# A graph network kernel: the stages between and behind the edge passes cut into chunks of four blocks

## The reference

```
h    = x @ node_fc_W + b ;  gate = sigmoid(x @ gate_W + gate_b)
# layer 0, per edge: attention over h[src] . h[dst], three relation weights from edge features,
# softmax by destination, segment sums, then a product with folded weights:
h_red = relu(concat([h_att, h_rel]) @ out_fc_W + out_fc_b)
h_out = where(deg > 0, h_red, h)
x1    = layernorm(x + gate * h_out + (1 - gate) * x)
# layer 1, per edge: e = tanh(x1[src] @ Wq + x1[dst] @ Wk), score = e @ Wphi,
# alpha = exp(score - max) / (sum over src + 1e-9)
out   = layernorm(x1 + segment_sum(alpha * (x1[dst] @ Wy_w + Wy_b + e @ We), src))
```

## Time and profile before

| | us |
|---|---|
| median of 3 runs | 2567.0 (2566.91 to 2568.18) |
| the profiled execution, its own time | 2568.5 |
| its span in the profile | 2566.9 |
| busy: PE / DVE / ACT / POOL | 2112.0 / 1811.4 / 1533.1 / 1658.5 |

### The profile page before, as it was taken

How to read it: one execution, slowest core, us unless ns; L and a number is a source line. 1 busy time by engine, 2 the same in 40 slices (tenths; PEclk the granted TensorE clock), 3 DMA queues, 4 the chain that set the end, 5 groups by cost and what they waited for, 6 DMA issues and landing times. The chain is left out here.

```text
span 2566.9 us, 63030 instructions
## 1 busy us (share of the span) xinstructions
PE 2112.0 (82%) x16604; PEld 1421.1 (55%) x16604; DVE 1811.4 (71%) x6215; ACT 1533.1 (60%) x4445; POOL 1658.5 (65%) x1800
## 2 busy tenths in 40 slices
PE   5799999997999999999995757777777777777773
PEld 4333333332677777777775446556555555555551
DVE  7984556110788888888876548787888887878764
ACT  2466777776666777667762136666666666666641
POOL 1277777776777777777720057777777777777740
PEclk9999999999899999999997558898989888989885
DMA  9244444553777777777731022222222222222220
GB/s 94 60 142 131 132 132 133 150 141 96 213 202 197 202 203 201 201 201 202 200 102 35 28 62 80 79 78 79 79 79 79 79 78 79 79 78 78 79 50 25
DMA packets 213904, 297.98 MB, mean 116 GB/s; under 512 B 87552, under 2 KB 136597, under 8 KB 213808
## 3 DMA queue, kind: packets, MB, share of 16 engines
q0 software_dynamic: 78400, 180.35, 25.9%
q1 hardware_dynamic: 135408, 116.54, 17.9%
HBM read 238.46 MB, written 58.28 MB: 116 GB/s over the span
## 5 line engine op out<-in xcount | busy, mean ns | idle before, releaser
L1569 POOL DMA_INDIRECT sum_acc<-kv_table,rec_all x784 | 741.4, 946 | 239.1 <-issue 236.6
L1068 POOL DMA_INDIRECT area_b<-h_table,src_g x448 | 459.1, 1025 | 144.0 <-issue 126.6
L512 POOL DMA_INDIRECT early<-h_table,src_g x336 | 331.3, 986 | 222.2 <-ACT sum_acc L727 141.8
L727 ACT ACTIVATE sum_acc<-twin,bias 128x1024 f32<-128x1024 f32 x294 | 318.1, 1118 | 154.9 <-PE twin L597 151.1
L1655 ACT COPY sum_acc<-sum_acc 128x768 f32 x220 | 183.4, 833 | 307.6 <-POOLq L1575 189.5
L597 PE MATMUL twin<-area_b,wc 64*128 64x512 f32 x1176 | 313.6, 634 | 11.0 <-ACT sum_acc L727 11.0
L1141 PE MATMUL bank<-hs,y_sb 128*128 128x129 f32 x2344 | 311.2, 275 | 0.6 <-ACT y_sb L1164 0.6
L1141 PEld LDWEIGHTS bank<-hs,y_sb 128*128 128x128 f32 x2344 | 285.7, 192 | 1.3 <-ACT y_sb L1164 1.1
L1168 ACT COPY y_sb<-bank 128x512 f32<-128x512 f32 x293 | 171.8, 586 | 190.6 <-PE bank L1132 190.6
L1627 PE MATMUL twin<-sum_acc,probT 128*128 128x193 f32 x880 | 206.9, 387 | 27.5 <-DVE probT L1765 27.0
L1627 PE MATMUL bank<-sum_acc,probT 128*128 128x193 f32 x880 | 206.0, 385 | 25.0 <-DVE probT L1765 23.4
(11 more groups left out here) (311 smaller groups left out, 4685.5 us busy)
## 6 DMA issues: line engine op xcount, KB each, us to landing
hs<-rows_table SPq DMA_DIRECT2D x293, 258.0 KB
rows_table<-area_b POOLq DMA_DIRECT2D x112, 258.0 KB
area_b<-in_edge_attr SPq DMA_DIRECT2D x97, 256.0 KB, 2.9
rows_table<-early POOLq DMA_DIRECT2D x84, 258.0 KB
sum_acc<-kv_table,rec_all POOLq DMA_INDIRECT x784
...
```

The costliest lines, as they stand in the source:

```text
L512: pool.indirect_dma_start(out=early[:, g % RINGE, j, 0:D], out_offset=None, in_=h_table, in_offset=bass.IndirectOffsetOnAxis(ap=src_g[:, g ...
L727: act.activation(hid_words[:, first:first + 2 * GE], twin[p % 2][:, :], ACT.Relu, bias=bias1[:, m:m + 1]).then_inc(hid_sb, 1)
L1068: pool.indirect_dma_start(out=landed_rows[:, g % RINGE * GT + j, 0:D], out_offset=None, in_=h_table, in_offset=bass.IndirectOffsetOnAxis(a ...
L1569: pool.indirect_dma_start(out=landed_rows[:, g % RING1 * GT + j, :], out_offset=None, in_=kv_table, in_offset=bass.IndirectOffsetOnAxis(ap ...
```

## The change

The middle and the last stage are written as loops over seven chunks: six of four blocks and one of a single block. Work with a factor or an offset per lane (h by `held`, relu by `taken`, x1 = y by rstd plus shift, the accumulator by den) becomes ACTIVATEs on ScalarE, one for each block with the factor as a pointer operand (128x1). gate is now computed in the first stage with a Tanh instead of the Sigmoid, and x_sb is multiplied there by 2 - gate. The value's bias moves out of the middle stage: it is row 65 of the weights w_e1 of the last stage, whose input is the 65 columns from D on of acc_st (the last is the sum of the weights), so the products with one row of ones are gone. rescale works on 8 windows instead of 20. kv_table is written by pairs of blocks from four buffers. The clears of acc_st and top_st stand on GpSimd in the middle stage. The last stage takes its maximum from the running maximum of the last step instead of searching for it, and writes the output chunk by chunk.

```diff
-w_e1 = sb("w_e1", [AD, D])
+w_e1 = sb("w_e1", [AD + 1, D])
...
-        (w_kvq[:, KV:], i["L1_gnn_Wq"]), (b_kvq[:, AD:KV], row(i["L1_gnn_Wy_b"])),
-        (w_e1[:, :], i["L1_gnn_We"]), (phi_b[:, :], i["L1_gnn_Wphi"].partition_broadcast(128)),
+        (w_kvq[:, KV:], i["L1_gnn_Wq"]), (w_e1[AD:, :], row(i["L1_gnn_Wy_b"])),
+        (w_e1[0:AD, :], i["L1_gnn_We"]), (phi_b[:, :], i["L1_gnn_Wphi"].partition_broadcast(128)),
...
+            act.activation(gate[:, :], gate[:, :], ACT.Tanh, scale=0.5).then_inc(gate_th, 1)
...
+    v.wait_ge(gate_th, 1)
+    step(v.tensor_scalar(gate[:, :], gate[:, :], 0.5, 0.5, ALU.mult, ALU.add))
+    step(v.tensor_scalar(rest[:, :], gate[:, :], -1.0, 2.0, ALU.mult, ALU.add))
+    step(v.tensor_tensor(x_sb[:, :, :], x_sb[:, :, :], rest[:, :].unsqueeze(2).to_broadcast([BN, NB, D]), ALU.mult))
...
+        if b >= CB and b % CB == CB - 1:
+            turn_x(b // CB - 1)
+            keys(b // CB - 1)
+    for c in (CHUNKS - 2, CHUNKS - 1):
+        turn_x(c)
+        keys(c)
...
+    def hold(c):
+        if c == 0:
+            act.wait_ge(h_in, 32)
+            act.wait_ge(weights, 1)
+        for b in blocks_of(c):
+            last = act.mul(h_all[:, b, :], h_all[:, b, :], held[:, b:b + 1])
+        last.then_inc(h_kept, 1)
+    def clip(c):
+        act.wait_ge(added, c + 1)
+        for b in blocks_of(c):
+            last = act.activation(y_sb[:, b, :], y_sb[:, b, :], ACT.Relu, scale=taken[:, b:b + 1])
+        last.then_inc(cut, 1)
+    def roots(c):
+        act.wait_ge(vars_in, c + 1)
+        act.activation(rstd[:, some_of(c)], rstd[:, some_of(c)], ACT.Sqrt).then_inc(vars_sq, 1)
+    def normalised(c):
+        act.wait_ge(shifts, c + 1)
+        for b in blocks_of(c):
+            last = act.activation(y_sb[:, b, :], y_sb[:, b, :], ACT.Identity, scale=rstd[:, b:b + 1], bias=shift[:, b:b + 1])
+        last.then_inc(x1_done, 1)
...
+    take_sums(0)
+    for c in range(CHUNKS):
+        for n, b in enumerate(blocks_of(c)):
+            if b + 1 < NB:
+                take_sums(b + 1)
+            if n == 1:
+                roots(c - 1) if c else hold(0)
+            if n == 2:
+                normalised(c - 1) if c else hold(1)
+        if len(blocks_of(c)) < 3:
+            roots(c - 1)
+            normalised(c - 1)
+        if c:
+            turned_x(c - 1)
+            take_keys(c - 1)
+        clip(c)
+        if c + 2 < CHUNKS:
+            hold(c + 2)
+    roots(CHUNKS - 1)
+    normalised(CHUNKS - 1)
+    turned_x(CHUNKS - 1)
+    take_keys(CHUNKS - 1)
...
-    step(v.scalar_tensor_tensor(y, y, 0.0, wide(has), ALU.max, ALU.mult))
-    v.wait_ge(h_in, 16)
-    step(v.tensor_tensor(h_all, h_all, wide(hasnt), ALU.mult))
-    step(v.tensor_tensor(y, y, h_all, ALU.add))
-    step(v.tensor_tensor(y, y, x_all, ALU.subtract))
-    step(v.tensor_tensor(y, y, wide(gate), ALU.mult))
-    step(v.scalar_tensor_tensor(y, x_all, 2.0, y, ALU.mult, ALU.add))
-    moments(v, y_sb, stats, mv, mean, rstd, per2)
-    v.sem_inc(vars_in, 1)
-    v.wait_ge(vars_sq, 1)
-    step(v.reciprocal(rstd[:, :], rstd[:, :]))
-    step(v.tensor_tensor(y, y, wide(mean), ALU.subtract))
-    step(v.tensor_tensor(y, y, wide(rstd), ALU.mult))
-    v.sem_inc(x1_all, 1)
-    for b in range(NB):
-        one = Chain(v, split_done, b * 5)
-        v.wait_ge(kvq_ps, b + 1)
...
+    def prepare(c):
+        v.wait_ge(h_kept, c + 1)
+        step(v.tensor_tensor(x_sb[:, some_of(c), :], x_sb[:, some_of(c), :], h_all[:, some_of(c), :], ALU.add))
+    def add_bias(c):
+        n = len(blocks_of(c))
+        v.wait_ge(out_ps, blocks_of(c)[-1] + 1)
+        v.tensor_tensor(y_sb[:, some_of(c), :], bank[3 + c % 2][:, 0:n * D].rearrange("p (b d) -> p b d", d=D),
+                        outb[:, :].unsqueeze(1).to_broadcast([BN, n, D]), ALU.add).then_inc(added, 1)
+    def finish(c):
+        y = y_sb[:, some_of(c), :]
+        v.wait_ge(cut, c + 1)
+        step(v.tensor_tensor(y, y, x_sb[:, some_of(c), :], ALU.add))
+        for n, b in enumerate(blocks_of(c)):
+            last = v.bn_stats(stats[:, n, :], y_sb[:, b, :])
+        step(last)
+        for n, b in enumerate(blocks_of(c)):
+            last = v.bn_aggr(mv[:, b, :], stats[:, n, :])
+        step(last)
+        v.tensor_scalar(rstd[:, some_of(c)], mv[:, some_of(c), 1], EPS, None, ALU.add).then_inc(vars_in, 1)
+    def spread(c):
+        v.wait_ge(vars_sq, c + 1)
+        step(v.reciprocal(rstd[:, some_of(c)], rstd[:, some_of(c)]))
+        v.scalar_tensor_tensor(shift[:, some_of(c)], mv[:, some_of(c), 0], -1.0, rstd[:, some_of(c)],
+                               ALU.mult, ALU.mult).then_inc(shifts, 1)
...
+    prepare(0)
+    for c in range(CHUNKS + 1):
+        if c + 1 < CHUNKS:
+            prepare(c + 1)
+        if c:
+            finish(c - 1)
+        if 2 * c + 4 < HALVES:
+            rescale(2 * c + 4)
+        if c:
+            spread(c - 1)
+        if 2 * c + 5 < HALVES:
+            rescale(2 * c + 5)
+        if c >= 2:
+            split(c - 2)
+        if c < CHUNKS:
+            add_bias(c)
+    split(CHUNKS - 1)
...
+    pool.memset(acc_st, 0.0).then_inc(cleared, 1)
+    pool.memset(top_st, NONE).then_inc(cleared, 1)
+    pool.wait_ge(cleared, 2)
...
-    pool.memset(acc_st, 0.0).then_inc(cleared, 1)
-    pool.memset(top_st, NONE).then_inc(cleared, 1)
...
+    act.activation(share[:, :], top_st, ACT.Exp, bias=neg_top[:, (STEPS - 1) % SU:(STEPS - 1) % SU + 1]).then_inc(shares, 1)
+    def scale(c):
+        for b in blocks_of(c):
+            last = act.mul(acc_st[:, b, :], acc_st[:, b, :], den[:, b:b + 1])
+        last.then_inc(acc_in, 1)
...
+    act.wait_ge(dens, 1)
+    scale(0)
+    scale(1)
+    for c in range(CHUNKS5):
+        turned(c)
+        if c:
+            roots(c - 1)
+        if c + 2 < CHUNKS5:
+            scale(c + 2)
+        if c:
+            normalised(c - 1)
+    roots(CHUNKS5 - 1)
+    normalised(CHUNKS5 - 1)
...
+    lift(0)
+    for c in range(CHUNKS5):
+        if c + 1 < CHUNKS5:
+            lift(c + 1)
+        if c:
+            spread(c - 1)
+        finish(c)
+    spread(CHUNKS5 - 1)
```

More of the change, by code:

```diff
@@ L1414, in take_keys @@
-                    def take_keys(b):
-                        act.wait_ge(kvq_ps, b + 1)
-                        act.copy(kv_b[:, b, :], bank[4 + 2 * (b % 2)][:, 0:KV]).then_inc(kv_sb, 1)
-                    turned_x(0)
-                    for b in range(NB):
-                        if b + 1 < NB:
-                            turned_x(b + 1)
-                        take_keys(b)
+                                 bank[b % 2][:, :].rearrange("d (w m n) -> d m w n", w=PER, m=M + 1)).then_inc(sum_sb, 1)
@@ L1842, in _ @@
+                    sp.wait_ge(stored, 16 * (-(-(NB - 1) // CB5) + 1))
                 @block.tensor
                 def _(pe):
[L1844 to L1855 removed]
@@ L1857, in outs @@
-                    def outs(s, k):
-                        b = s * W + k
-                        pe.wait_ge(e_sb, b + 1)
-                        if not is_first(b):
-                            pe.wait_ge(added, b)
-                        pe.matmul(bank[3][0:BN, 0:D], eT_b[:, k, :], w_e1[:, :], start=True, stop=True).then_inc(out_ps, 1)
-                    def body(s, k, edge):
-                        if inside(edge, k, 1, W):
-                            turn(*step_of(s, k, 1, W))
-                        if inside(edge, k, 0, W):
-                            outs(s, k)
@@ L1869, in _, with turn, outs @@
-                    rounds(pe, body, 1, NB, W)
+                    def turn(c):
+                        pe.wait_ge(acc_in, c + 1)
+                        if c >= 2:
+                            pe.wait_ge(e_sb, c - 1)
+                        for n, b in enumerate(blocks_of(c)):
+                            last = pe.transpose(bank[c % 2][0:AD + 1, n * BN:(n + 1) * BN], acc_st[:, b, D:KV + 1], identf[:, :])
+                        last.then_inc(e_ps, 1)
+                    def outs(c):
+                        pe.wait_ge(e_sb, c + 1)
+                        if c >= 2:
+                            pe.wait_ge(added, c - 1)
+                        for n, b in enumerate(blocks_of(c)):
+                            last = pe.matmul(bank[2 + c % 2][:, n * D:(n + 1) * D], eT[:, c % 2, n * BN:(n + 1) * BN], w_e1[:, :],
+                                             start=True, stop=True)
+                        last.then_inc(out_ps, 1)
```

331 lines of the change are left out of this document (168 added, 163 removed).

## The result

| | before | after |
|---|---|---|
| median | 2566.95 (4 runs, 2565.59 to 2568.18) | 2477.85 (4 runs, 2477.47 to 2478.42) |
| span of the profiled execution | 2566.9 | 2476.8 |

A forecast was written before the change was run, and what follows sets the result against it. Bound: GpSimd's gathers in the second edge pass, untouched; in the middle and last stages, the order of work. Terms -43.9 - 4.2 - 35.0 + 0.2 = -82.9 us, 2568.5 to 2485.6 profiled, median 2484; range 2464 to 2501.

The forecast's parts named there:

- Relay, then ring: Middle stage: engines worked in turn before; after, chunks run one after another, clip waiting for the previous chunk's keys; -43.9 us.
- The size of a round: Middle stage: one chunk's turn, from the end of hold to the end of the next, 14.0 us (11 to 16.5).
- The rival with cheap pointers: Middle and last stage: pointer operands cost nothing and TensorE runs at full clock, so shorter rounds; 2468 us; 20%.
- Start: Middle stage: hold(0) waits for both loads, rec_all landing 9.5 us after issue; VectorE passes beside the clear cost nothing.
- the rival of 3%: GpSimd's clears delay VectorE or are not hidden; +4.2 us, 2488; 3%.
- The clear ahead of the gathers: Before the second edge pass: clears move into the middle stage, first gather 0.2 us after the small clear, not 4.4; -4.2.
- One-row products: Middle stage: dropping one single-row matmul pair per block takes 0.94 us off TensorE's period, 25 x 0.94 = 23 us.
- Last stage: After the second edge pass: chunked work without the maximum search takes 37.5 us against 72.5; -35.0.
- The gather pace: Second edge pass: stays 1.251 us per gather; slower rival, each gather taking longer, 2586 us at 0.13 more; 2%.
- The clock stayed up: Middle and last stage: the rival said TensorE's clock stays down, +2.05 us per round over six; 2498 us; 15%.
- True overlap: Middle stage: rival that chunks truly overlap, VectorE's 8.3 us being the round; 2452 us; 8%.
- The rule against it: Middle stage: the skill keeps relu and mul on VectorE; moving them to ScalarE loses 8.5 us, already in the sum.

The follow-up runs named there:

- e4: Changed kernel with hold's product moved from ScalarE to VectorE, one 128x512 instruction per chunk; 2473.52 us, rounds 10.8.
- e5: Changed kernel with hold and clip both on VectorE, each one 128x512 instruction per chunk; 2456.79 us, rounds 12.4 and then 9.06.
- e1: Changed kernel with ScalarE doing clip(c) and hold(c + 2) ahead of turned_x(c - 1) and take_keys(c - 1) in the middle stage; 2474.76 us.
- e6: Changed kernel with GpSimd's clears held back until the sixth chunk is normalised; 2479.81 us.
- e2: Changed kernel with the clears of acc_st and top_st put back on GpSimd ahead of the first gather; 2482.7 us.
- e10: Kernel before without its one-row products (value's bias left out), run on a chip with slower gathers; ratio to before 0.9903.
- e8: Changed kernel with a one-row product of zeros put back behind each keys product, 25 in all; 2509.1 us.

## Why the prediction was right, point by point

- **Relay, then ring.** Right. ScalarE's clip is right behind L1471 in each full round, the chunks go one after another, and e4 and e5, and e1 where its clock is full, shorten the round by what they take out of it, once TensorE's place in the ring is counted.
- **The size of a round: 14.0 forecast, 12.6 measured.** Prepare and add 1.46, normalise 1.65 (1.6 said), transposes and eviction 1.3, keys 2.86 (2.95), clip and hold 1.2 and 1.2: all right. Off were statistics, 1.5 and not 2.05 (I scaled the old loop, which idles 0.25 at its head and copies the mean besides), reciprocal and shift (0.2 less), and the clock: TensorE was granted 1.00 in the rounds from 1377.6 to 1424, so the 0.65 for it was not needed. Over the three full rounds that is -4.2, over the next two -2.7; with +1.6 at the start and +1.1 behind these rounds, 0.5 of it GpSimd's idle time ahead of the first gather, it makes the 4.3 us between -48.1 and -52.4. Two counts beside the sum don't come out: TensorE's busy time adds up to 8.2 and not 8.6 (8.9 measured), and of VectorE's 125 split passes 21 are left, not 50.
- **Pointer operands.** One pointer: four ACTIVATEs in 1.28 of 0.389 each, 0.30 apart; two: 1.65, 0.479, 0.39 apart. The Trainium skill (ScalarE: Activation LUTs, What ACT_TABLE_LOAD costs) states about 93 ns for each pointer operand, and the trace agrees (0.479 - 0.389 = 0.09). The rival with cheap pointers was wrong in its reason, though the ring was shorter.
- **Start.** The forecast had hold(0) at 10.4 behind the load's issue and the end of the third hold at 19.65 (its terms add up to 19.5); measured 11.9 and 21.3. The step that failed: "they fall in the time before rec_all lands: nothing". The clear held VectorE's first instruction for 4.2 us, and 1.6 came through (e6). The Trainium skill (SBUF — State Buffer, SBUF: two separate sides) has this rule: a GpSimd instruction and some of VectorE's take a shared pair of ports, and whoever starts second waits for the whole of the other. The trace agrees, 4.20 for 0.25 beside a clear of 4.13. So the rival of 3% (the clears delay VectorE) did happen, at 1.6 and not 4.2. That taking the clear away won nothing at the first gather was the clock's doing.
- **The clear ahead of the gathers, -4.2.** 3.6 by e2: the first gather comes 0.66 behind the small clear and not 0.2. The pace of 1.251 carried all of it to the end.
- **One-row products, 0.94 us each, 23 us.** The removal alone is 26.7 (e10): the period falls to 1.35, not 1.47, where VectorE's five small passes set it. What the forecast didn't see is that the same products would have cost even more in the new layout (28.7, e8): it priced their place in the old row of work, and half of the middle stage's gain would be missing had they stayed.
- **Last stage, 37.5 forecast, 34.8 measured** from its first instruction. First chunk 9.5 (9.65 said); 3.8 a chunk instead of 4.2; the end 6.2 instead of 6.9. Statistics are 0.5 shorter there too; what the rest of these differences is wasn't taken apart. The sign "VectorE the busiest" was wrong: ScalarE is busy for 24.5 of the 34.8 us and VectorE for 20.6.
- **Rivals.** The gather pace didn't move. The clock stayed up in the ring and down in the last stage (0.54), as assumed. True overlap didn't happen by itself, but e5 shows it was there to be had: 2456.8, near the 2452 priced for it, with TensorE's 9.06 as the round and not VectorE's 8.3. Some of the total's closeness is luck: the rounds were 6.9 us shorter than forecast, and 2.7 of that were covered by what was longer around them (the start and the end of the stage), another 1.6 by the pass and its last group.
- **The rule against it** ("relu and mul on VectorE"). It was worth more than the 8.5 us that I priced: e5 follows it for hold and clip, and its stage is 18.5 us shorter (its median 21). That isn't a matter of elements per us. One pass of 0.69 replaces four starts that take 1.28 together, 2 x 0.6 a round, but the round fell by 3.5; so most of it should be that the work left the queue on which the evictions wait. No run separates the two, so this split is argued from the rows.
